# Mixture-of-experts results stored in slot order and gathered by token, with rings of six for the expert tiles

## What is computed

```python
gu = x @ shared_gate_up_w.T;  g, u = split(gu)
shared = sigmoid(x @ shared_gate_w.T) * ((silu(g) * u) @ shared_down_w.T)
top_w, top_i = top_k(softmax(x @ gate_w.T), 2)          # 2 of 8 experts
combine[t, top_i] = top_w / sum(top_w)
ge, ue = split(einsum('th,eih->tei', x, w1))
ye = einsum('tei,ehi->teh', silu(ge) * ue, w2)
out = einsum('teh,te->th', ye, combine) + shared
```

## Time and profile before

| | us |
|---|---|
| median of 3 runs | 590.56 (588.28 to 592.87) |
| span of the profiled execution | 596.5 |
| tile stage from the sixth `tile_in` to its end, f0 / f1 | 57.0 / 57.0 |
| from there to the end of the block, f0 | 24.4 |
| from there to the end of the span, f1 | 22.5 |

### The profile page before, as it was taken

The page is one execution under the profiler, slowest core; times in us unless marked ns, Lnnn a source line. Parts: engine busy times, 40 slices in busy tenths (PEclk is TensorE's granted clock), DMA queues, the critical chain, the costliest instruction groups (busy, mean ns, idle before and its releaser), DMA issues. The chain is left out here.

```text
span 596.5 us, 10712 instructions
## 1 busy us (share of the span) xinstructions
PE 536.5 (90%) x3359; PEld 466.1 (78%) x3360; DVE 339.5 (57%) x822; ACT 273.4 (46%) x731; POOL 271.4 (46%) x358
## 2 busy tenths in 40 slices
PE   7769797889799999999999999999998869888797
PEld 3558686778588998889988889888897648777687
DVE  5797633328876465564655646556466595433337
ACT  3636544343165264552645526455263534443441
POOL 2358466652334454444544445544432231566630
PEclk9979899999899999999999999999999999999999
DMA  6525422224300201002010020100000410222235
GB/s 222 168 71 162 132 93 85 88 79 151 80 1 1 72 0 49 23 0 70 0 47 24 0 70 0 48 22 0 0 0 0 132 37 19 72 87 90 79 106 168
DMA packets 19912, 37.99 MB, mean 64 GB/s; under 512 B 2864, under 2 KB 11440, under 8 KB 19888
## 3 DMA queue, kind: packets, MB, share of 16 engines
q1 hardware_dynamic: 15472, 25.62, 13.6%
q0 software_dynamic: 4416, 12.06, 5.9%
HBM read 28.50 MB, written 9.18 MB: 63 GB/s over the span
## 5 line engine op out<-in xcount | busy, mean ns | idle before, releaser
L1261 POOL TENSOR_TENSOR s_a<-s_a,rr_a 128x128 f32<-128x128 f32 x64 | 25.7, 401 | 136.3 <-DVE rr_a L1358 136.3
L1297 ACT ACTIVATE s_a<-s_a,mn_a 128x128 f32<-128x128 f32 (+1 forms) x128 | 57.1, 448 | 27.7 <-DVE mn_a L1352 26.8
L499 POOL DMA_INDIRECT rows_f<-x_normed,tok_i_f x46 | 45.8, 995 | 49.4 <-PE bank L1027 30.1
L171 PE MATMUL bank<-xT_h,area_h 128*128 128x512 f32 x128 | 56.3, 440 | 2.5 <-PEq L1128 2.5
L1364 DVE SCALAR_TENSOR_TENSOR area_l<-bank,bias_a,area_h 128x256 fp32r<-128x256 f32 x64 | 30.9, 483 | 42.7 <-ACT area_h L1307 42.7
L505 POOL DMA_INDIRECT y_by_token<-rows_f,place_f x46 | 45.5, 988 | 19.6 <-issue 11.6
L1348 DVE SCALAR_TENSOR_TENSOR s_a<-bank,cst 128x384 f32<-128x384 f32 x64 | 35.3, 552 | 33.3 <-PE bank L1472 33.3
L172 PE MATMUL bank<-xT_l,area_h 128*128 128x512 f32 x128 | 51.2, 400 | 0.0
L173 PE MATMUL bank<-xT_h,area_l 128*128 128x512 f32 x128 | 51.0, 399 | 0.0
L171 PE MATMUL bank<-w_h,xeT_h_f 128*128 x92 | 34.4, 374 | 17.9 <-DVE xeT_l_f L787 15.5
L1307 ACT ACTIVATE area_h<-bank,bias_a 128x256 fp32r<-128x256 f32 x64 | 30.3, 473 | 42.2 <-PE bank L1500 41.1
(11 more groups left out here) (174 smaller groups left out, 1677.5 us busy)
## 6 DMA issues: line engine op xcount, KB each, us to landing
area<-in_wqkv SPq DMA_DIRECT2D x8, 768.0 KB, 4.3
xn<-y_by_token SPq DMA_DIRECT2D x12, 256.0 KB, 3.0
area<-in_w SPq DMA_DIRECT2D x8, 352.0 KB
area<-in_w SPq DMA_DIRECT2D x16, 176.0 KB
x_normed<-xn SPq DMA_DIRECT2D x4, 512.0 KB, 3.7
area<-in_wo SPq DMA_DIRECT2D x8, 256.0 KB
x_res<-in_x_in SPq DMA_DIRECT2D x4, 256.0 KB, 4.4
area<-in_wgu SPq DMA_DIRECT2D x4, 256.0 KB
```

Of the source, the lines that this page charges most:

```text
L171: pe.matmul(psum, lhs[0], rhs[0], start=first, stop=False)
L499: pool.indirect_dma_start(xe[m % 2], None, xd, bass.IndirectOffsetOnAxis(ap=tok_i[:, m:m + 1], axis=0)).then_inc(s_xe[m % 2], 16)
L1297: act.activation(s[b][:, cols], s[b][:, cols], ACT.Exp, bias=mn[:, b, t:t + 1], scale=-1.0, accum_out=rs[:, b, t:t + 1]).then_inc(s_e, 1)
```

## The change

- The ring of gathered tiles has six buffers, slices 0 to 5 of `xn`; `gather(m)` waits until tile m-6 is transposed.
- The ring of results has six buffers: the four slices of `rows` and slices 6 and 7 of `xn`. `tile_out(m)` waits until the store of tile m-6 has landed.
- The scatter is gone. SP stores each result tile by a plain DMA, 128 rows in slot order, into `y_by_slot`.
- When all stores have landed, POOL gathers the rows by token with 16 indirect DMAs, two for each token tile, in place of SP's eight loads. The first 12 stand ahead of the layer norm's `norm_rstd` in POOL's order in f0, the last four behind it; those also wait for the adds of token tiles 0 and 1.
- The splits of the attention weights on POOL stand ahead of these gathers.
- The first add moves one chunk later (`ADDS`).
- ACT's two-step loop is written out. PE's loop stays at six steps, DVE's at two. The semaphores of the rings count on through both blocks.

```diff
-ADDS = (0, 0, 0, 1, 1, 1)
+ADDS = (0, 0, 0, 0, 1, 1)
-OUT_LAG = 6
+XR = 6
+YR = 6
...
-                xe, ye = [[rows[:, a + b, :] for b in range(2)] for a in (0, 2)]
-                lgT = xe + ye
+                lgT = [rows[:, a, :] for a in range(4)]
+                xe = [xn[:, b, :] for b in range(XR)]
+                ye = lgT + [xn[:, b, :] for b in range(XR, NT)]
...
+                def ring_uses(m, depth):
+
+                    return (0 if first else -(-(NM - m % depth) // depth)) + m // depth
...
+                    for m in range(NM):
+                        sp.wait_ge(s_ye, m + 1)
+                        sp.dma_start(yd[m * P:(m + 1) * P, :], ye[m % YR]).then_inc(s_yst[m % YR], 16)
...
                     def gather(m):
-                        if m >= 2:
-
-                            pool.wait_ge(s_tx, m - 1)
+                        if m >= XR:
+
+                            pool.wait_ge(s_tx, m - XR + 1)
...
                     if after:
                         for t in range(3):
                             attention_low(pool, t)
-                        norm_rstd(pool, after, 0)
+                    for b in range(YR):
+                        pool.wait_ge(s_yst[b], 16 * ring_uses(b + (NM - 1 - b) // YR * YR, YR) + 16)
+                    for j in range(NT):
+                        if after and j == NT - 2:
+                            norm_rstd(pool, after, 0)
+                        if Y_BUF[j] in Y_BUF[:j]:
+
+                            pool.wait_ge(s_add, pair_added(Y_BUF.index(Y_BUF[j])))
+                        for t in range(TOP_K):
+                            pool.indirect_dma_start(
+                                y_buf(j)[:, t, :], None, yd,
+                                bass.IndirectOffsetOnAxis(ap=slot_i[:, t * NT + j:t * NT + j + 1], axis=0)
+                                ).then_inc(s_y[Y_BUF[j]], 16)
...
+                        if m >= YR:
+
+                            act.wait_ge(s_yst[m % YR], 16 * ring_uses(m, YR))
+                        act.activation(ye[m % YR][:, :], bank[6 + b][:, 0:D], ACT.Copy).then_inc(s_ye, 1)
```

More of the change, by code:

```diff
@@ L143, in macaron @@
         y_in = [0] * 6
+        s_xe = [sem(f"s_xe{b}") for b in range(XR)]
+        s_yst = [sem(f"s_yst{b}") for b in range(YR)]
         QKV = 3 * KD * 2 * DH
@@ L327, in ffn @@
                 s_dnv = sem(f"s_dnv_{tag}")
-                s_xe = [sem(f"s_xe{b}_{tag}") for b in range(2)]
                 s_tx = sem(f"s_tx_{tag}")
@@ L339, in ffn @@
                 s_ye = sem(f"s_ye_{tag}")
-                s_yst = [sem(f"s_yst{b}_{tag}") for b in range(2)]
                 s_add = sem(f"s_add_{tag}")
                 s_out = None if first else sem("s_out")
+                def ring_uses(m, depth):
+                    return (0 if first else -(-(NM - m % depth) // depth)) + m // depth
                 jobs = []
@@ L512, in _ @@
                                 job_low(pool, q, s_wlp)
-                        if m < NM:
-                            gather(m)
-                        if m >= OUT_LAG:
-                            scatter(m - OUT_LAG)
+                        gather(m)
                     if after:
@@ L606, in inner_silu, with tile_out @@
                         act.activation(he[b][:, :], bank[2 + b][:, 0:IM], ACT.Silu).then_inc(s_es, 1)
[L608 removed]
+                    def tile_out(m, b):
                         act.wait_ge(s_ed, m + 1)
[L610 to L638 removed]
+                        if m >= YR:
+                            act.wait_ge(s_yst[m % YR], 16 * ring_uses(m, YR))
+                        act.activation(ye[m % YR][:, :], bank[6 + b][:, 0:D], ACT.Copy).then_inc(s_ye, 1)
+                    for m in range(NM + 2):
+                        if 0 < m + 1 < NM:
+                            tile_high(m + 1, (m + 1) % 2)
+                        if m < NM:
+                            inner_silu(m, m % 2)
+                        if 0 < m <= NM:
+                            inner_high(m - 1, (m - 1) % 2)
+                        if m >= 2:
+                            tile_out(m - 2, m % 2)
                     if after:
@@ L1021, in _, with tile_in @@
                         shared_up(c)
-                    def tile_in(m, q, b):
-                        pe.wait_ge(s_xe[b], 16 * (q + 1))
+                    def tile_in(r, b, q=0):
+                        pe.wait_ge(s_xe[r % XR], 16 * (ring_uses(r, XR) + q + 1))
                         for k in range(KD):
-                            last = pe.transpose(bank[b][:, k * P:(k + 1) * P], xe[b][:, k * P:(k + 1) * P], ident)
+                            last = pe.transpose(bank[b][:, k * P:(k + 1) * P],
+                                                xe[r % XR][:, k * P:(k + 1) * P], ident)
                         last.then_inc(s_tx, 1)
@@ L1073, in down, with step @@
                         last.then_inc(s_ed, 1)
-                    def step(m, q, b, guard=True):
-                        tile_in(m + 1, q + b, 1 - b)
+                    def step(m, r, b, guard=True, q=0):
+                        tile_in(r + 1, 1 - b, q)
                         up(m, b)
@@ L1084, in _ @@
                     pe.wait_ge(s_hm, SC + AHEAD - 1)
-                    tile_in(0, 0, 0)
-                    tile_in(1, 0, 1)
+                    tile_in(0, 0)
+                    tile_in(1, 1)
                     pe.wait_ge(s_hm, SC + AHEAD)
@@ L1098, in _ @@
                     next_experts(1)
-                    tile_in(2, 1, 0)
+                    tile_in(2, 0)
                     up(1, 1)
@@ L1104, in _ @@
                     wait_low(pe, len(jobs) - 1)
-                    step(2, 1, 0, False)
-                    step(3, 1, 1, False)
-                    assert (NM - 5) % STEPS == 0
+                    step(2, 2, 0, False)
+                    step(3, 3, 1, False)
+                    assert (NM - 5) % STEPS == 0 and STEPS == XR
                     with pe.Fori(0, (NM - 5) // STEPS) as i:
                         for k in range(STEPS):
-                            step(STEPS * i + 4 + k, STEPS // 2 * i + 2 + k // 2, k % 2)
+                            step(STEPS * i + 4 + k, 4 + k, k % 2, q=i)
                     m = NM - 1
```

49 lines of the change are left out of this document (6 added, 43 removed).

## The result

| | before | changed kernel |
|---|---|---|
| median of 20 timed runs | 588.69 us (586.13 to 592.87) | 591.25 us (588.92 to 595.64) |
| ratio, 95% interval | | 1.0048 (1.0028 to 1.0068) |
| span of the profiled execution | 596.5 us | 588.6 us (its own time 590.47) |
| forecast | | 586.6 us (579 to 599) |

The range holds the result, the direction is wrong: the forecast was a gain of 4 us, and the change costs 0.5%. The two spans say the opposite, 7.9 us saved. By it the span of before, 596.5, belongs to a time of about 598.4, and none of its 20 timed runs took more than 592.87.

What follows compares the result with a forecast made beforehand. Took PE's gaps in the tile stages to come from POOL's indirect-DMA queue and the two-buffer rings. −26.2 (stages) + 11.1 + 10.6 (tails) + 0.5 (clock) = −4.0 us, so 590.56 becomes 586.6 us, range 579 to 599.

Steps and rivals of the forecast that it cites:

- tile stages: Tile loops of f0 and f1: 18 steps at 2.2 us make 43.9 us instead of 57.0, saving 26.2 us in both.
- tail f0: Behind f0's tiles: 16 gathers, the last four behind the layer norm, end 35.5 us after the tiles instead of 24.4, losing 11.1.
- tail f1: Behind f1's tiles: 16 gathers, no split or norm, 33.0 us to the span's end instead of 22.5, losing 10.6.
- between: Attention's start, between the blocks: PE idles some 7 us before it and starts at half clock, charged 0.5 us more.
- an extra idle of 0.9 us ahead of every fourth: POOL's indirect DMAs in the tile stages: a pause taken as the queue's own, within a 6.04 us period per two tiles.
- The chain to PE runs through the other ring: Tile stage: ACT's `tile_out` waits 4.57 us for a scatter's landing, delaying DVE's low part and PE's `up`.
- The first gather: Behind the tiles: first gather by token starts 5.2 us after `shared_up` starts (T) in f0, 3.4 us after in f1.
- The cadence: Gathers by token on POOL: 1.4 us from one to the next; each 0.1 us is worth 2.5 us.
- The landing: Gathers by token: 3.7 us from start until PE or DVE can use the rows; each 0.5 us is worth 1.5 us.
- Everything at its best edge: Rival for whole kernel: cadence 1.27, landing 2.84, step 2.13 us give 8.4 us more gain, 578.2 us; chance 0.25.
- The gathers by token become the bound: Rival behind the tiles: gathers 1.78 us apart beside DVE's work, landing 4.49 us, total 598.5 us; chance 0.20.
- The tile stage does not reach PE's rate: Rival in tile stages: PE's steps stay at 2.62 us, gain shrinks by 15.1 us, total 601.7 us; chance 0.07.

Runs made afterwards that it cites:

- e1: The kernel before, unchanged, profiled a second time, without the pause: 587.26 us, ratio to itself 0.9944.
- e7: The kernel before, unchanged, profiled a third time, with the pause: 600.66 us beside 604.38, ratio 0.997.
- e15: The changed kernel, unchanged, run where before shows the pause: 605.71 us, 1.0044 of before.
- e2: The changed kernel with its rings of six, but results scattered by POOL and loaded by SP as before: 585.06 us, 0.9901 of before.
- e13: The kernel of e2 with each scatter ten places behind its gather in POOL's queue instead of six, with the pause: 599.82 us, 0.9939 of before.
- e3: The changed kernel with both rings cut back to two buffers: 591.75 us, 1.0041 of before.
- e4: The changed kernel with SP's eight plain loads from the slot table in place of the 16 gathers by token (rows reach wrong tokens): 576.67 us.
- e16: The changed kernel with a small POOL instruction behind each gather by token, with the pause: 597.50 us, 0.9883 of before.
- e6: The changed kernel with eight gathers by token in place of 16, each token's second row left out, run where before pauses: 582.42 us.
- e11: The kernel of e3 with a second, idle gather of the same rows behind each tile's gather from the third tile on: 633.91 us.
- e9: The changed kernel, unchanged, run where before shows the pause: 603.73 us, 0.9972 of before.
- e14: The changed kernel, but POOL waits before each pair of gathers by token until the pair two before has landed, with the pause: 602.08 us, 0.9995.
- e17: The kernel of e13 with a small POOL instruction behind each scatter and each gather from the tenth on, with the pause: 598.98 us, 0.991.

## Why the prediction was wrong

Term by term, against e1, the profile of before in the rhythm of the timed comparison, and against e7 and e15, both with the pause:

| term | forecast | without the pause (e1 to changed) | with it (e7 to e15) |
|---|---|---|---|
| tile stages | −26.2 | −5.5 − 6.0 = −11.4 | −12.8 − 13.6 = −26.4 |
| tail f0 | +11.1 | +8.4 | +13.8 |
| tail f1 | +10.6 | +7.7 | +13.9 |
| between | +0.5 | +0.4 | +0.8 |
| sum | −4.0 | +5.1 | +2.1 |

The timed difference is +2.6 us. The sum of the profiles without the pause is 2.5 us above it, which single executions allow: with the start of the program, 2.4 us shorter in the changed kernel's, the two spans differ by 2.6 us.

**The step that failed** is in the first part of the prediction: "an extra idle of 0.9 us ahead of every fourth. The cause that the profile names for it (`tile_in`, 87.85) had long been over, so I take it as the queue's own". The pause is not always there. The 57.0 us of a tile stage were taken as a property of the kernel, and in the timed comparison a stage took 49.3. That is 15.4 of the 26.2 us; the other terms as forecast would then have given 10.8 us of gain against 22.2 of loss, 11 us slower; the tails came out cheaper, and so it was 2.6. (Nor, probably, is the pause "the queue's own": by the last section it looks like POOL's wait for PE, met late.) The page had the warning: the span lay 5.9 us above the median and 3.6 above the highest time then known, 592.87, though a span must lie below its own time. The prediction subtracted differences in place of asking what was different.

In the rhythm that the prediction did read the stage term is right (−26.4 for −26.2), and there the tails are what failed: +27.7 for +21.7, because DVE stood for up to 12.8 us, and PE behind it, while gathers were issued that the prediction had counted only at their own length.

A second step failed with the first: "The chain to PE runs through the other ring", the wait of `tile_out` for a scatter's landing. Six buffers in place of two took 1.0 us off a stage (e1 to e2), and in e13 the same wait of ACT, 2.71 us, stands where the ring has not come round and no landing is waited for.

**What held.** The stage of the changed kernel: 43.8 and 43.3 for 43.9, with `tile_in` 2.20 us apart on the mean in f0. The first gather at T + 5.1 for T + 5.2, in f1 at T + 3.1 for T + 3.4; the last four behind the norm; half clock at attention's start (0.52 for 0.59 before); the stretch between the blocks, where 0.5 us was charged for it, is 0.4 us longer, but it differs by 0.8 us among e3, e4 and the changed kernel, so this shows nothing.

**What was too dear.** The cadence was taken as 1.4 us, midway between 1.27 and the 1.51 of the pause, and is 1.34 over the first seven intervals of f0, 1.32 over its last three and 1.30 over the 15 of f1: 2.2 us in all. The landing was taken as 3.7 us and is 3.4, 2.8 and 3.2 where it decides, 1.7 us in all. Together they are most of the 5.5 us by which the tails are shorter. For the landing, the profile lists a median of 2.8 us. The estimate by the Trainium skill ("DMA: Bandwidth & Descriptors", "Anatomy of one DMA") was 2.3 us: the trace disagrees, by 0.5 to 1.1 us. It was somewhat further off than the 3.7 us that I took, and nearer than the 4.49 us that I held against it.

**The rivals.** *Everything at its best edge* had the tails about right and failed on the same base. *The gathers by token become the bound* was right in its heading and not in its mechanism: they do set both tails (e4: 14.8 us), but at 1.30 to 1.34 us, not 1.78. A gather beside DVE's work is longer by 0.1 to 0.2 us (1.08 at 134.19, 0.95 else), not by the 0.5 of the earlier trace rows. By the Trainium skill ("SBUF — State Buffer", "Who interferes with whom") a DVE instruction with two SBUF inputs contends with a GpSimd instruction that reads SBUF, and the contention is an exclusive lock. Blocked for the whole of DVE's 0.7 to 0.9 us a gather would be longer by up to as much; 16 gathers beside DVE's adds and low parts show far less. *The tile stage does not reach PE's rate* is refuted by 43.67 of 43.82 us. The rival that decided was not among them: that the gap to be closed is smaller in the runs that count than in the one that was read.

**What stays open.** What holds PE's signals in the one rhythm and not in the other; whether rings of six with scatters ten behind reach 577 us without it; and why the part between the blocks is 2 to 5 us longer in the kernels with rings of six and scatters (364.6 to 367.8 us against 361.9 in e1 and 363.0 in e7).

No version was shown to beat both kernels in both rhythms. Without the pause e2 did (585.1 beside 588.8, of which half can be chance by e1); with it e16 did, the changed kernel with its gathers spaced (597.5 beside 603.1).

## What to carry to other kernels

Before working from a profiled execution, put its span beside the timed runs: a span above the highest time does not come from an execution like those that are timed, and its idle times may be its own. Where two limits seem to vanish together (a ring and a queue), count the queue's work for each step first (2 × 1.28 against 2.2 us here); it tells which one holds without any experiment. Work that is moved from a stage where an engine has slack to behind it must be fewer instructions than what covers it there: eight gathers were free in f1 (e6), sixteen cost 7 us (the changed kernel against e4).

## What the runs showed of the hardware that was not expected

- The same kernel takes some 588 or 603 us, and what differs between the traces is the rhythm of POOL's indirect DMAs: 1.28 us each, or 1.51 on the mean with a pause (e1, e7). It was the same for all that ran beside each other, and chip number 13 showed both.
- The pause comes with gathers alone too, when there are two for each tile (e11), and does not show in the changed kernel's tile stage, with one for each 2.1 to 2.5 us (e9: 44.0 and 43.9 us).
- In the rhythm with the pause, what PE tells the other engines seems to reach them late while POOL issues indirect DMAs. In e13 ACT's copy of tile 3 waits for PE's `down` alone (its ring has not yet come round), which ended at 81.39 + 0.28; ACT starts at 84.04, 0.9 us after POOL's scatter was issued (82.17 + 0.99). POOL's gather of 84.32 waits for the transposes of tile 7, done by 81.9. So the pause of POOL looks like its own wait for PE, held as the others are; no run separates this from a pause that POOL makes by itself and the others follow. Behind the tiles, where 16 gathers follow each other, the hold grows to 12.8 us, ends in f1 1.7 to 2.6 us after POOL stops, and is gone with a POOL instruction of 0.2 us between them (e9, e14 to e16); in the tile stage the same instruction only moves the pauses (e17).

PE, ACT, POOL and DVE in e13:

```profile
81.39 0.28 PE L176 MATMUL bank<-area_h,heT_l_f 88*128 x1
...
84.04 0.38 ACT L621 ACTIVATE rows_f<-bank 128x256 f32<-128x256 f32 x1 [2.71 <-PE bank L176]
...
82.17 0.99 POOL L512 DMA_INDIRECT y_by_token<-rows_f,place_f  x1 [0.30 <-issue]
84.32 0.96 POOL L506 DMA_INDIRECT xn<-x_normed,tok_i_f  x1 [1.17 <-PE bank L1021]
...
84.73 0.42 DVE L780 TENSOR_TENSOR xeT_l_f<-bank,xeT_h_f 128x256 fp32r<-128x256 f32 x1 [2.95 <-issue]
```

DVE is late only because ACT's high part stands behind its copy, as in the earlier trace rows.
